# Recurrent layer of a four-layer kernel: the forget gate in a PSUM bank of its own and first in order, output rows summed by GpSimd, the state product's two waits swapped

## The reference, cut to what matters

```python
def step(carry, xp):                       # xp = x @ W_ih + b_ih + b_hh
    h, c = carry
    gates = xp + h @ W_hh.T
    i, f, g, o = jnp.split(gates, 4, axis=-1)
    c = jax.nn.sigmoid(f) * c + jax.nn.sigmoid(i) * jnp.tanh(g)
    h = jax.nn.sigmoid(o) * jnp.tanh(c)
    return ((h, c), h)
...
logits = jnp.einsum('bth,lh->btl', lstm_out, W_lin) + b_lin
g = argmax(logits, axis=-1)[..., None]     # 0 or 1 for each row
w = g * lstm_out
inc = jnp.cumsum(w, axis=1)
return 2.0 * lstm_out + (inc - w) * fw_att + (inc[:, -1:, :] - inc) * bw_att
```

## Time and profile before

| | |
|---|---|
| median of 3 runs | 4451.14 us (4450.52 to 4453.53) |
| span of the profiled execution | 4442.7 us (first to last instruction; the profile has no other time of it) |
| recurrent layer in it | from about 2942 to 4366 us, then a tail of 77 us |
| TensorE, VectorE, ScalarE, GpSimd busy | 3984.7, 3491.9, 2883.5, 1183.3 us |

### The profile page before, as it was taken

How to read it: one execution, slowest core, us unless ns; L and a number is a source line. 1 busy time by engine, 2 the same in 40 slices (tenths; PEclk the granted TensorE clock), 3 DMA queues, 4 the chain that set the end, 5 groups by cost and what they waited for, 6 DMA issues and landing times. The chain is left out here.

```text
span 4442.7 us, 143559 instructions
## 1 busy us (share of the span) xinstructions
PE 3984.7 (90%) x55713; PEld 2856.6 (64%) x55713; DVE 3491.9 (79%) x9562; ACT 2883.5 (65%) x7050; POOL 1183.3 (27%) x1032
## 2 busy tenths in 40 slices
PE   7999999996999999999997999978888888888882
PEld 5666666653665666666665777767777777777772
DVE  6999999985889889888986888846666666666666
ACT  6999999985888888888884777733333333333330
POOL 4777877762222222222221101100000000000000
PEclk9999999998999999999998999999999999999996
DMA  2222221210000000000002433411111111111115
...
DMA packets 327039, 251.03 MB, mean 57 GB/s; under 512 B 172889, under 2 KB 291033, under 8 KB 324313
## 3 DMA queue, kind: packets, MB, share of 16 engines
...
## 5 line engine op out<-in xcount | busy, mean ns | idle before, releaser
L2578 PE MATMUL lstm_G_psum<-next_Whh,lstm_HT 128*32 128x192 f32 x8192 | 439.8, 332 | 254.9 <-DVE lstm_HT L2710 254.9
L2649 ACT ACTIVATE lstm_TC<-lstm_G_psum 128x192 f32<-128x192 f32 x512 | 169.9, 332 | 690.7 <-PE lstm_G_psum L2578 690.7
L1565 ACT ACTIVATE ssm_EX<-ssm_Z_psum,ssm_tok 128x256 f32<-128x256 f32 (+1 forms) x1024 | 372.6, 424 | 155.2 <-PE ssm_Z_psum L1396 85.5
L2578 PEld LDWEIGHTS lstm_G_psum<-next_Whh,lstm_HT 128*32 128x32 f32 x8192 | 213.9, 109 | 340.3 <-DVE lstm_HT L2710 306.8
L2570 PE MATMUL lstm_G_psum<-next_Wih,lstm_XT 128*32 128x192 f32 x8192 | 427.7, 327 | 0.0
L2697 DVE SCALAR_TENSOR_TENSOR lstm_AB<-lstm_TC 128x128 f32<-128x128 f32 x512 | 149.6, 292 | 290.2 <-ACT lstm_TC L2649 289.0
L616 ACT ACTIVATE g_PR<-g_S,g_nmax 128x512 f32<-128x512 f32 x512 | 368.4, 723 | 4.0 <-DVE g_nmax L751 4.0
L758 DVE COPY g_PT<-g_PT_psum 128x512 f32<-128x512 f32 x512 | 344.4, 684 | 24.0 <-PE g_PT_psum L485 19.3
L607 ACT ACTIVATE g_relu<-g_Z_psum,g_src 128x512 f32<-128x512 f32 x512 | 347.0, 685 | 17.5 <-PE g_Z_psum L478 17.4
L2872 POOL TENSOR_SCALAR lstm_rstd<-lstm_mv 128x4 f32<-128x4 f32 x32 | 7.2, 226 | 1310.0 <-DVE lstm_mv L2691 1310.0
L751 DVE CUSTOM_DVE_ANT_0 g_S<-g_Z_psum,g_relu 128x512 f32<-128x512 f32 x512 | 345.4, 684 | 8.4 <-ACT g_relu L607 6.9
...
## 6 DMA issues: line engine op xcount, KB each, us to landing
...
lstm_U<-x SPq DMA_DIRECT2D x128, 128.0 KB, 3.4
lstm_V<-lstm_U SPq DMA_DIRECT2D x128, 128.0 KB, 3.3
```

Source lines behind the costliest of these rows:

```text
L1565: ins = act.activation(EX[h % NE][:, col:col + n], Zb[c][:, i * CHUNK:i * CHUNK + n], ACT.Exp, bias=tok[b.slot][:, i, c, h:h + 1])
L2578: ins = pe.matmul(bank[32 * j:32 * (j + 1), 0:last - first], HT[t % 2][:, 32 * kc:32 * (kc + 1)], Whh[:, kc, j, first:last], start=False, ...
```

## The change

- The gates are computed in the order f, then i and g together, then o. f has one bank F, o has one bank O (both reused at every step), i and g share G[0] or G[1]. Each gate group picks its columns out of the weights. The inputs of the next step wait for the tanh of f and of o of this step, for i and g of the step before.
- ScalarE has four operations a step: tanh of f into TF (64 columns), of i and g into IG (128), of o into TO (64), and of the cell state.
- VectorE makes KP = (f + 1) C, then IN = (i + 1) g, then C = 0.5 KP + IN, each of 64 columns, then H. H waits first for tc and then for TO.
- The ten operations on the output rows of all blocks but the last are GpSimd's: `own` twice, ahead of `scales`, the other eight behind it. `counted` runs once a step at t = 3 to 6 and twice at t = 8 to 13. `move` on SP waits for the sixth operation on U itself.
- `normalised` comes after t = 9 and 10.

```diff
-        Ob = [m.ps(f"O{k}") for k in range(2)]
+        Fb = m.ps("F")
+        Ob = m.ps("O")
...
+        def rows(c, hf):
+            return U[c.slot][:, HALF * hf:HALF * (hf + 1), :]
+
+        def own(eng, c, hf):
+            c.wait(eng, s["h"], S, S)
+            if hf == 0:
+                c.dma_wait4(eng, resid)
+            eng.tensor_tensor(rows(c, hf), rows(c, hf), H[c.slot][:, HALF * hf:HALF * (hf + 1), :], ALU.add
+                              ).then_inc(s["u"], 1)
+
+        def before_it(eng, c, hf):
+            c.wait(eng, s["inc"], S + 1, HALF * (hf + 1) + 1)
+            c.wait(eng, s["u"], 6, 4 if hf else 0)
+            eng.tensor_tensor(part[:, :, :], inc[:, HALF * hf:HALF * (hf + 1), :],
+                              fw[:, :].unsqueeze(1).to_broadcast([P, HALF, HB]), ALU.mult).then_inc(s["part"], 1)
+
+        def before_added(eng, c, hf):
+            c.wait(eng, s["part"], 4, 2 * hf + 1)
+            c.wait(eng, s["u"], 6, 2 + 2 * hf)
+            eng.tensor_tensor(rows(c, hf), rows(c, hf), part[:, :, :], ALU.add).then_inc(s["u"], 1)
+
+        def up_to_it(eng, c, hf):
+            c.wait(eng, s["u"], 6, 2 + 2 * hf + 1)
+            eng.tensor_tensor(part[:, :, :], inc[:, HALF * hf + 1:HALF * (hf + 1) + 1, :],
+                              bw[:, :].unsqueeze(1).to_broadcast([P, HALF, HB]), ALU.mult).then_inc(s["part"], 1)
+
+        def up_to_taken(eng, c, hf):
+            c.wait(eng, s["part"], 4, 2 * hf + 2)
+            eng.tensor_tensor(rows(c, hf), rows(c, hf), part[:, :, :], ALU.subtract).then_inc(s["u"], 1)
...
-                c.wait(sp, s["done"], 1, 1)
+                c.wait(sp, s["u"], 6, 6)
...
+        def of_gate(ap, gate):
+
+            parts_of = ap.rearrange("p (a b e) -> p a b e", a=2, b=2)
+            return {"ig": parts_of[:, :, 0, :], "f": parts_of[:, 0, 1, :], "o": parts_of[:, 1, 1, :]}[gate]
+
+        def into(gate, t, j):
+
+            rows_of = slice(32 * j, 32 * (j + 1))
+            if gate == "ig":
+                return Gb[t % 2][rows_of, 0:2 * HB].rearrange("p (a e) -> p a e", a=2)
+            return (Fb if gate == "f" else Ob)[rows_of, 0:HB]
...
-                for bank, first, last, read in ((Gb[t % 2], 0, IFG, s["tg"]), (Ob[t % 2], IFG, 4 * HB, s["to"])):
-                    c.wait(pe, read, S, t - 1)
-                    n = last - first
+                for gate in ("f", "ig", "o"):
+                    if gate == "f":
+                        c.wait(pe, s["tf"], S, t)
+                    if gate == "ig":
+                        c.wait(pe, s["tg"], S, t - 1)
+                    if gate == "o":
+                        c.wait(pe, s["to"], S, t)
                     for j in range(J):
-                        pe.matmul(bank[32 * j:32 * (j + 1), 0:n], ones_bf[:, :],
-                                  bias[:, 4 * HB * j + first:4 * HB * j + last],
+                        pe.matmul(into(gate, t, j), ones_bf[:, :], of_gate(bias[:, 4 * HB * j:4 * HB * (j + 1)], gate),
                                   start=True, stop=False, skip_group_check=True)
                     for kc in range(KC):
                         for j in range(J):
-                            pe.matmul(bank[32 * j:32 * (j + 1), 0:n], XT[c.slot][:, kc, :, t],
-                                      Wih[:, kc, j, first:last], start=False, stop=False, skip_group_check=True)
+                            pe.matmul(into(gate, t, j), XT[c.slot][:, kc, :, t], of_gate(Wih[:, kc, j, :], gate),
+                                      start=False, stop=False, skip_group_check=True)
 
             def hidden(c, t):
-                for bank, first, last, made in ((Gb[t % 2], 0, IFG, s["g"]), (Ob[t % 2], IFG, 4 * HB, s["go"])):
+                for gate, made in (("f", s["gf"]), ("ig", s["g"]), ("o", s["go"])):
                     for kc in range(KC):
                         c.wait(pe, s["ht"], KC * S, KC * t + kc + 1)
                         for j in range(J):
-                            ins = pe.matmul(bank[32 * j:32 * (j + 1), 0:last - first],
-                                            HT[t % 2][:, 32 * kc:32 * (kc + 1)], Whh[:, kc, j, first:last],
-                                            start=False, stop=(kc == KC - 1), skip_group_check=True)
+                            ins = pe.matmul(into(gate, t, j), HT[t % 2][:, 32 * kc:32 * (kc + 1)],
+                                            of_gate(Whh[:, kc, j, :], gate), start=False, stop=(kc == KC - 1),
+                                            skip_group_check=True)
                     ins.then_inc(made, 1)
...
             def gates(c, t):
+                c.wait(act, s["gf"], S, t + 1)
+                c.wait(act, s["keep"], S, t)
+                act.activation(TF[:, :], Fb[:, 0:HB], ACT.Tanh).then_inc(s["tf"], 1)
                 c.wait(act, s["g"], S, t + 1)
-                c.wait(act, s["ab"], S, t - 1)
-                act.activation(TC[t % 2][:, 0:3, :].rearrange("p g e -> p (g e)"), Gb[t % 2][:, 0:IFG], ACT.Tanh
+                c.wait(act, s["inp"], S, t)
+                act.activation(IG[:, :, :].rearrange("p g e -> p (g e)"), Gb[t % 2][:, 0:2 * HB], ACT.Tanh
                                ).then_inc(s["tg"], 1)
                 c.wait(act, s["go"], S, t + 1)
-                c.wait(act, s["h"], S, t - 1)
-                act.activation(TO[t % 2][:, :], Ob[t % 2][:, 0:HB], ACT.Tanh).then_inc(s["to"], 1)
+                c.wait(act, s["h"], S, t)
+                act.activation(TO[:, :], Ob[:, 0:HB], ACT.Tanh).then_inc(s["to"], 1)
 
             def cell(c, t):
                 c.wait(act, s["c2"], S, t + 1)
-                act.activation(tc[:, :], TC[(t + 1) % 2][:, 3, :], ACT.Tanh, scale=0.5).then_inc(s["tc"], 1)
+                act.activation(tc[:, :], C[:, :], ACT.Tanh, scale=0.5).then_inc(s["tc"], 1)
...
-                    if nxt and t in (8, 9):
-                        normalised(c + 1, 2 * (t - 8))
-                        normalised(c + 1, 2 * (t - 8) + 1)
+                    if nxt and t in (9, 10):
+                        normalised(c + 1, 2 * (t - 9))
+                        normalised(c + 1, 2 * (t - 9) + 1)
...
             def step(c, t):
+                c.wait(v, s["tf"], S, t + 1)
+                c.wait(v, s["c2"], S, t)
+                v.scalar_tensor_tensor(out=KP[:, :], in0=TF[:, :], scalar=1.0, in1=C[:, :], op0=ALU.add, op1=ALU.mult
+                                       ).then_inc(s["keep"], 1)
                 c.wait(v, s["tg"], S, t + 1)
-                c.wait(v, s["c2"], S, t)
-                v.scalar_tensor_tensor(out=AB[:, :, :], in0=TC[t % 2][:, 0:2, :], scalar=1.0, in1=TC[t % 2][:, 2:4, :],
-                                       op0=ALU.add, op1=ALU.mult).then_inc(s["ab"], 1)
-                c.wait(v, s["ab"], S, t + 1)
-                v.scalar_tensor_tensor(out=TC[(t + 1) % 2][:, 3, :], in0=AB[:, 1, :], scalar=0.5, in1=AB[:, 0, :],
+                v.scalar_tensor_tensor(out=IN[:, :], in0=IG[:, 0, :], scalar=1.0, in1=IG[:, 1, :], op0=ALU.add,
+                                       op1=ALU.mult).then_inc(s["inp"], 1)
+                c.wait(v, s["inp"], S, t + 1)
+                c.wait(v, s["keep"], S, t + 1)
+                v.scalar_tensor_tensor(out=C[:, :], in0=KP[:, :], scalar=0.5, in1=IN[:, :],
                                        op0=ALU.mult, op1=ALU.add).then_inc(s["c2"], 1)
+                c.wait(v, s["tc"], S, t + 1)
                 c.wait(v, s["to"], S, t + 1)
-                c.wait(v, s["tc"], S, t + 1)
-                v.scalar_tensor_tensor(out=H[c.slot][:, t, :], in0=TO[t % 2][:, :], scalar=1.0, in1=tc[:, :],
+                if t == 0:
+                    c.wait(v, s["u"], 6, 2 - 2 * 6)
+                v.scalar_tensor_tensor(out=H[c.slot][:, t, :], in0=TO[:, :], scalar=1.0, in1=tc[:, :],
                                        op0=ALU.add, op1=ALU.mult).then_inc(s["h"], 1)
                 c.wait(v, s["h"], S, t + 1)
...
                 c.wait(v, s["repp"], 1, 1)
+                c.wait(v, s["part"], 4, 0)
                 v.tensor_copy(gS[:, :], LGb[c.slot][:, REP_AT:REP_AT + S]).then_inc(s["gs"], 1)
...
             def beside(c, t):
 
                 if t == 1:
                     choose(c)
-                    own(c, 0)
                 if t == 2:
                     gate_out(c)
-                    own(c, 1)
-                if 3 <= t <= 7:
-                    counted(c, 2 * (t - 3))
-                    counted(c, 2 * (t - 3) + 1)
-                if t == 8:
-                    before_it(c, 0)
-                    counted(c, 10)
-                if t == 9:
-                    before_added(c, 0)
-                    counted(c, 11)
-                if t == 10:
-                    up_to_it(c, 0)
-                    counted(c, 12)
-                if t == 11:
-                    up_to_taken(c, 0)
-                    counted(c, 13)
-                if t == 12:
-                    counted(c, 14)
-                    counted(c, 15)
```

(23 more changed lines are left out.)

53 lines of the change are left out of this document (14 added, 39 removed).

## The result

The changed kernel takes 4793.27 us (median of 4 runs, 4782.70 to 4799.42), the kernel before 4451.65 (4 runs, 4450.52 to 4453.53): 1.0764 times as long, 95% interval 1.0750 to 1.0779, or 342 us more. Forecast were 4540 us and a range of 4455 to 4640. The direction was right and the size was not: 253 us are missing from the sum. The profiled execution has a span of 4794.5 us at a mean granted clock of 0.967.

What follows compares the result with a forecast made beforehand. The prediction took a ring of engines handing on one item, 2.755 us a step, as the bound. It summed -100 us without the part on GpSimd and +189 us for GpSimd's sums to 4540 us, range 4455 to 4640.

Steps and rivals of the forecast that it cites:

- the sum: Whole kernel: -100 us without the part on GpSimd, +189 us for its sums, +89 us on the 4442.7 us span.
- TensorE's new order: TensorE's gate matmuls: i and g ready when they are now; second input part adds 0.06 us a step, covered by idle time.
- a ring of 2.57 us: Recurrent layer: engines hand one item round each time step; 2.755 us before, 0.188 a step less, 96 us over 512 steps.
- what would show it: Closing list of timeline signs: most steps at 2.57 us, those with GpSimd at work at 3.5 to 4.0 if right.
- T0: Start of TensorE's state matmuls in a step; i and g were forecast ready 0.86 us after it.
- Rivals 3 and 5: 3: f first not free on TensorE, 4673 us, chance 0.06; 5: swapping leaves H's start, 4573 us, within the forecast's 0.68.
- the swap: VectorE's two waits before H, late one written first: H starts sooner, gain 0.065 us a step, bounds 0 and 0.065.
- The exclusion: VectorE operations with two SBUF inputs wait out 1.00 us of each GpSimd sum: 6.1 us a block, 189 us.
- Rival 1: VectorE and GpSimd: no exclusion between operations this small, the gain stands, 4351 us; chance 0.10.
- rival 2: VectorE and GpSimd: half the exclusion, if GpSimd's starts fall where VectorE is idle, 3.05 us a block, 4446 us; chance 0.09.
- Rival 4: TensorE's clock falls after idle time in stretched steps: three hit a block, 60 us, 4600 us; chance 0.07.
- The normalisation: ScalarE's work for the next block, one step later: GpSimd's shift is ready by then, gain 6 us.

Runs made afterwards that it cites:

- the kernel with 152 instructions: The changed kernel, sums still on GpSimd, with the bias products and the second half of the input products left out: 4567.14 us, 1.0265.

## Why the prediction was right, and where it failed

**The step that failed is "TensorE's new order", with its sentence "the columns are the same".** It counted columns and idle time and not instructions. The split of one bank's group in two adds 32 instructions to the state products, 32 to the input products and 8 to the bias, since every product in f32 shows as two matmuls with a load each: 152 to 224 a step. It priced the extra part on the input side at 0.06 us, covered by 0.56 of idle time. That time is there (0.28 us idle ahead of 3826.55, and the state products wait for HT), but the limit is elsewhere: 224 / 256 x 3.80 = 3.33 us a step against a ring of 2.57. The size: 377 us where the sums are on VectorE (4733.53 - 4356.93), 226 us on top of the sums (4793.27 - 4567.14). The second is the term that is missing from the sum, and it makes up nearly all of the 253 us; the other 27 are sized below. By "what would show it", steps near 2.8 where GpSimd rests were to say that TensorE's order costs. They are longer still: from start to start of the state products, the median over the blocks of the steps t = 3 and 4, where GpSimd rests, is 3.52 and 3.50.

It could have been read before. The earlier trace rows have 39095 + 39087 instructions in 1424 us, 4.66 us for 256; at 224 a step and the ring as forecast the chip would have had to bring 256 in 256 / 224 x 2.57 = 2.9 us, and none of the rows read shows that. A rate 1.6 times the one shown was taken for free; its other end belonged into the range.

**The ring was right.** 2.58 against 2.57 forecast. i and g: their tanh starts at 3824.90, 0.93 after the start of the state products, against 3508.72 - 3507.80 = 0.92 in the earlier trace rows; so T0 + 0.86 for the matmuls holds, and f first is free (its tanh at T0 + 0.49, KP at T0 + 0.75, as forecast). IG takes 280 ns (276 forecast), IN and C 0.23 and 0.22. H starts 0.032 behind the end of tc (the median of the 512 steps), where 0.035 was forecast and 0.102 was before. Rivals 3 and 5 fall. In all -93 us measured where -100 was forecast; the swap gives 0.065 a step of it, as both kernels with the swap alone show (2.755 to 2.69).

**The exclusion was right in kind and near in size.** The sums cost +210 us in the new ring against 189 forecast, but 40 of these are the clock's (below), so the exclusion is some 170, a tenth less than forecast. The hold on 64-column operations ends 0.15 us before the sum does, forecast 0.13. Rival 1 (no exclusion) and rival 2 (half) fall. The power operation with its 4 columns, which spoke for rival 1, did not say anything on a sum of 512. By the Trainium skill ("SBUF — State Buffer", section "Who interferes with whom") the second of the two is blocked for the whole of the first; the exclusion is confirmed, the whole isn't, neither for two inputs (released 0.15 before the end) nor for one (0.43 of 1.50).

**Rival 4, the falling clock, came beside the forecast** and not in its place: 1.51 for 0.86 us after 2.76 of idle time, a layer at 0.93 in the kernel with 152 instructions and 0.96 in the changed one. The rival had three steps a block hit, 60 us; it is 64 steps in 30 blocks and 40 us in the new ring, and one step a block and 21 us in the old. The sum had it at nothing. That the kernel with 152 instructions came within 27 us of 4540 is in part luck: the ring gained 7 us less than forecast, the exclusion cost some 19 less and the clock 40 more. What the clock costs in the changed kernel was not separated from the stops.

**Exclusion and supply don't add.** The sums cost 211 us alone and 60 beside the supply limit. What fits is that TensorE's next instructions come in while VectorE waits for GpSimd, so that the two overlap; fewer stops in the changed kernel (289, 258 us) than in the one with the sums on VectorE (431, 377 us) bear that out. A sum over parts cannot show it.

**The normalisation**, one step later: forecast 6 us, measured some 25 beside the swap (16.0 us gained without it, 40.8 with it), since without it the swap runs into the shift operation that VectorE holds up.
